# A pairwise attention pooling kernel: Gram rows written 58 wide from a second ScalarE copy, in four DMAs a block in place of eight

## The reference

```
row, col = np.triu_indices(F, k=1)              # 741 pairs of 39 fields
ip = x[:, row, :] * x[:, col, :]                # (B, 741, 64)
hidden = relu(einsum('bpd,da->bpa', ip, W_w) + b_w)
logits = einsum('bpa,a->bp', hidden, W_h) + b_h[0]
a = softmax(logits, axis=1)[:, :, None]
return sum(a * ip, axis=1) @ W_p + b_p          # (2048, 1), float32
```

## Time and profile before

| | |
|---|---|
| median of 3 runs | 1045.51 us (1042.35 to 1046.46) |
| the profiled execution | 1050.66 us, of which the span of the core's instructions is 1048.9 us |
| TensorE busy | 1032.0 us (98%) |
| VectorE busy | 981.7 us (94%) |
| ScalarE busy | 870.6 us (83%) |
| GpSimd busy | 420.5 us (40%) |
| granted TensorE clock | 0.998 of full |
| DMA packets, bytes | 413979, 45.63 MB |

### The profile page before, as it was taken

One profiled execution on the slowest core, in us unless ns is written; L12 is line 12 of the kernel. 1 busy time (PEld: TensorE's weight loads), 2 busy tenths in 40 slices (PEclk: granted clock), 3 DMA queues, 4 the chain that ended last, 5 costly groups with the idle time before them and its releaser, 6 DMA issues.

```text
span 1048.9 us, 59118 instructions
## 1 busy us (share of the span) xinstructions
PE 1032.0 (98%) x24849; PEld 481.6 (46%) x24849; DVE 981.7 (94%) x549; ACT 870.6 (83%) x884; POOL 420.5 (40%) x263
## 2 busy tenths in 40 slices
PE   7999999999999999999999999999999999999997
PEld 3445444444554445544455554544444544444542
DVE  8999999999999999999999999999999989999992
ACT  6888887888888888888888888888888888888885
POOL 6253433452334433535333335333433445342331
PEclk9999999999999999999999999999999999999999
DMA  3242243422434234242342523325253242422422
GB/s 52 40 51 43 36 49 42 47 42 37 49 47 49 36 47 47 39 55 32 48 47 35 61 32 50 42 34 59 35 50 47 31 53 40 50 41 37 47 34 26
DMA packets 413979, 45.63 MB, mean 44 GB/s; under 512 B 413915, under 2 KB 413931, under 8 KB 413931
## 3 DMA queue, kind: packets, MB, share of 16 engines
q1 hardware_dynamic: 413611, 45.12, 33.9%
q10 hardware_dynamic: 320, 0.07, 0.0%
HBM read 26.59 MB, written 18.54 MB: 43 GB/s over the span
## 4 chain that ended last, share of the span: by engine, by line
PE 97%; DVE 1%; issue 1%; ACT 0%; DMA 0%; another core or an unknown queue 0%; ACTq 0%; DVEq 0%
PE z L513 61%; PE logits L563 32%; PE z L502 5%; DVE prod L348 1%; DMA first_x_rows<-in_r_x_dram 0%; ACT hidden L431 0%; ACT exps L454 0%; PE logits L553 0%; DVE neg_max L357 0%; DVE weighted L365 0%; PE z L493 0%; PE z L627 0%; DVE x_wide L330 0%; DVE y_all L371 0%
## 5 line engine op out<-in xcount | busy, mean ns | idle before, releaser
L431 ACT ACTIVATE hidden<-z,b_col 128x988 f32<-128x988 f32 x768 | 803.5, 1085 | 149.2 <-PE z L513 145.6
L348 DVE TENSOR_TENSOR prod<-x_wide 128x2964 f32<-128x2964 f32 (+1 forms) x257 | 822.4, 3246 | 2.1 <-PE z L513 1.2
L513 PE MATMUL z<-prod,w_tiles 64*32 64x494 f32 x12288 | 760.4, 576 | 0.3 <-ACT hidden L431 0.2
L292 POOL COPY head_w<-head_cols 128x64 f32<-128x64 f32 x252 | 408.8, 1624 | 604.2 <-PE logits L563 604.0
L563 PE MATMUL logits<-hidden,head_w 64*32 64x371 f32 (+1 forms) x8192 | 442.3, 472 | 5.5 <-PE logits L563 1.8
L513 PEld LDWEIGHTS z<-prod,w_tiles 64*32 64x32 f32 x12288 | 251.1, 106 | 263.6 <-issue 232.7
L563 PEld LDWEIGHTS logits<-hidden,head_w 64*32 64x32 f32 x8192 | 179.1, 106 | 245.5 <-issue 233.9
L319 DVE STREAM_TRANSPOSE x_wide<-x_rows 128x1024 f32<-128x1024 f32 x63 | 78.5, 1246 | 24.4 <-PE z L502 19.1
L502 PEld LDWEIGHTS z<-x_wide,x_scaled 64*39 64x39 f32 x4096 | 45.0, 113 | 40.1 <-issue 40.1
L439 ACT COPY gram_out<-z 103x624 f32<-103x624 f32 x64 | 43.5, 680 | 16.5 <-PE z L502 14.9
L502 PE MATMUL z<-x_wide,x_scaled 64*39 64x39 f32 x4096 | 52.5, 204 | 1.1 <-DVE prod L348 0.6
(11 more groups left out here) (27 smaller groups left out, 29.0 us busy)
## 6 DMA issues: line engine op xcount, KB each, us to landing
x_rows<-in_r_x_dram SPq DMA_DIRECT2D x252, 64.0 KB
gram<-gram_out SPq DMA_DIRECT2D x256, 47.5 KB
gram<-gram_out SPq DMA_DIRECT2D x256, 23.2 KB
values<-gram SPq DMA_DIRECT2D x128, 46.3 KB, 3.5
x_rows<-in_r_x_dram SPq DMA_DIRECT2D x252, 14.0 KB
first_x_rows<-in_r_x_dram SPq DMA_DIRECT2D x2, 78.0 KB
first_x_rows<-in_r_x_dram SPq DMA_DIRECT2D x1, 156.0 KB
w_tiles<-in_L_rec_W_w_dram ACTq DMA_DIRECT2D x4, 16.0 KB, 2.9
```

The costliest lines, as they stand in the source:

```text
L292: nc.gpsimd.tensor_copy(head_w[:, step % BLOCK_STEPS, :, :], head_cols[:, :, at:at + TILE]).then_inc(head_w_ready, 1)
L348: nc.vector.tensor_tensor(out, one, other, ALU.mult).then_inc(ready, 1)
L431: nc.scalar.activation(hidden[:, i, :, CHUNK * k:CHUNK * (k + 1)], z[:, slot_of(j, v), :, 0:CHUNK], ACT.Relu, bias=b_col[:, 0:1]).then_inc ...
L513: last = nc.tensor.matmul(z[col:col + TILE, slot_of(j, v), b, 0:CHUNK], w_tiles[row:row + D, col:col + TILE], prod[row:row + D, i, first:f ...
```

## The change

`gram_out` gets rows of 58 in place of 39. `copy_gram` writes the 39 columns as before and then takes the first 19 of each matrix out of PSUM once more, in a second ScalarE instruction (103 partitions x 304 elements); `z_read` is raised by the second. `write_gram` issues one DMA of rows of 58 for each quarter, 4 a block, and the counts that wait for them go by 4.

```diff
-        gram_out = sb("gram_out", [P, 2, 2, ROW_DUOS, FIELDS])
+        gram_out = sb("gram_out", [P, 2, 2, ROW_DUOS, WIDE])
...
-        GRAM_DMAS = 8
+        GRAM_DMAS = 4
...
-                        rows = gram_blocks[h, u, :, bass.ds(v, 1), :, :]
-                        sp.dma_start(rows[:, :, :, 0:FIELDS],
+                        sp.dma_start(gram_blocks[h, u, :, bass.ds(v, 1), :, :],
                                      gram_out[at:at + FIELDS, slot, u, :, :]).then_inc(gram_written[slot], 16)
-                        sp.dma_start(rows[:, :, :, FIELDS:WIDE],
-                                     gram_out[at:at + FIELDS, slot, u, :, 0:OFFSETS]).then_inc(gram_written[slot], 16)
...
-                nc.scalar.copy(gram_out[0:ROWS, slot, :, :, :],
-                               z[0:ROWS, GRAM_SLOT, :, 0:XCOLS].rearrange("p u (d f) -> p u d f", f=FIELDS)
-                               ).then_inc(z_read, 1)
+                taken = z[0:ROWS, GRAM_SLOT, :, 0:XCOLS].rearrange("p u (d f) -> p u d f", f=FIELDS)
+                nc.scalar.copy(gram_out[0:ROWS, slot, :, :, 0:FIELDS], taken)
+                nc.scalar.copy(gram_out[0:ROWS, slot, :, :, FIELDS:WIDE], taken[:, :, :, 0:OFFSETS]).then_inc(z_read, 1)
```

## The result

The changed kernel takes 1040.35 us (median of 20 runs, 1038.79 to 1042.09), the kernel before 1042.76 us (median of 20 runs beside them, 1041.08 to 1046.46). The ratio is 0.9974, 95% interval 0.9968 to 0.9980: 2.4 us, a quarter of a percent, faster. Two things add up to the miss of 5.2 us. The level was wrong by 2.7 us, since the median of three runs (1045.51) was high for this kernel; and the effect, forecast as 0, was 2.4 us.

What follows compares the result with a forecast made beforehand. TensorE, busy 98% of the span, was taken to bound the kernel. Every term counted 0 on its path, so the forecast was 1045.5 us, no change, with a range of 1041 to 1050 us.

Steps and rivals of the forecast that it cites:

- The level: Starting time without the profiler, median of three runs: 1045.51 us, to which the change's effect of 0 was added.
- The second ScalarE copy: Added 64 times after the Gram copy: 0.42 us each, fits ScalarE's idle hole before chunk 2's relu, costs 0 on the path.
- the 0.39 us ahead of chunk 5: TensorE's slack at chunk 5, which waits for chunk 3's relu: 530.70 against a start at 531.09 us.
- the 20 us of the sum: ScalarE's added busy time from the second copies, overlap taken off: 64 x (0.42 - 0.11) us.
- The sign of 897 us: What would show the forecast right: ScalarE's busy time up by about 27 us to 897 us.
- The first copy: The 39 columns written into rows of 58 with gaps: 0 extra, at most 0.16 us more, still inside the slack.
- Four DMAs less on SyncE: Four fewer Gram write issues a block, x loads 1.8 us sooner; nobody waits for them, gain 0, loss 0.
- the 333700 of the prediction: Sign of a right forecast: queue 1, the data queue, at about 333700 packets.
- Fewer packets: Gram writes from 159744 to 79872 packets; DMA share 27% to 34%, not on the chain, effect 0.
- two windows: Two neighbouring blocks, 15.83 us each at DMA shares 0.57 and 0.26, taken as showing DMA doesn't press on TensorE.
- Rival 2: Faster: TensorE's stalls were DMA's; half of the 14.2 us gone gives 1038.4 us, all 1031.3 us. Chance 7%.
- 14.2 us: Group openings and stalls between first and last Gram copy, beyond 63 steady blocks: the most a change of waits could give back.

Runs made afterwards that it cites:

- wide_4_no_copy: The changed kernel without the second ScalarE copy, columns 39 to 57 of gram_out zeroed once at the start: 1040.63 us, ratio 0.9873.
- wide_8_halves: The changed kernel with each of the 4 whole-row DMAs cut into two of half as many batches, 8 issues a block: 1040.31 us, ratio 0.9872.
- before_x_sooner: The kernel before with SyncE's order changed, x loads placed between two halves of a block's eight Gram writes: 1041.33 us, ratio 0.9882.
- split_4_apart: The kernel of wide_4_split_rows with its 116 B packets 128 B apart in DRAM in place of end to end: 1040.44 us, ratio 0.9872.
- wide_4_split_rows: The changed kernel, 4 DMAs a block, with every row of 58 sent as two 116 B packets end to end in DRAM: 1132.96 us, ratio 1.0759.
- only_39: The kernel before without the four DMAs of 19 columns, leaving 79872 packets of 156 B at 232 B steps: 1040.04 us, ratio 0.9887.
- narrow_8_pitch_64: The kernel before with DRAM rows 64 floats (256 B) apart in place of 58 (232 B), still 8 DMAs: 1040.30 us, ratio 0.9867.
- copy_kept_8_narrow: The changed kernel, second copy kept, with the writes as before: 8 DMAs a block, runs of 39 and 19: 1052.73 us, ratio 0.9998.
- before_pe_by_4: The kernel before with TensorE's loop over single blocks replaced by one over groups of four blocks: 1192.96 us, ratio 1.1326.

## Why the prediction was wrong, by its steps

**The second ScalarE copy: right.** 0.42 us, in the hole, 0 on the path; wide_4_no_copy has the same time as after. The relu behind it started at its old distance of 1.17 us from chunk 2 in every block, so the 0.39 us ahead of chunk 5 weren't touched. ScalarE's busy time went up by the 20 us of the sum, to 890.3 us. The sign of 897 us at the end of the prediction contradicts that sum, as it counts 64 x 0.42 us without the overlap.

**The first copy: right.** Gaps cost 10 ns (0.69 for 0.68 us).

**Four DMAs less on SyncE: right for whole rows.** Eight or four issues, x loads early or late make no difference there (wide_8_halves, after). With the narrow rows of before the order of the issues is worth 13 us (before_x_sooner). The queue has 330411 packets and not the 333700 of the prediction: each of the 256 issues left out took 13 packets of 4 B with it, 3328 in all, and wide_8_halves, which kept its issues, has 333739.

**Fewer packets: this step failed.** "I take 0 from both ends" rested on two windows with the same 15.83 us at a DMA share of 0.57 and of 0.26. They showed that in these two blocks the loads of `values` didn't disturb TensorE. They did not show that the Gram writes don't, as both blocks contain those, and both happened to be undisturbed. Traffic was weighed by its share of the engines, where kind and place mattered: split_4_apart and wide_4_split_rows have the same packets by number and size, and are 92 us apart. What stood in the place of this 0: with two narrow packets a row at 232 B steps, written by eight DMAs in one go, single x packets take up to 0.8 us and TensorE has late starts; with whole rows there are no such packets, and one late start is left. That is 11 us of late starts in the profiled execution, 2.4 us by the medians of 20 runs, and 10 to 14 us in the later sets.

**Rival 2** was nearest to what happened, with 7%: the late starts were of DMA's making. Its reason (half of the packets) holds only at this step of rows: only_39, with half of the packets, is fast, but so is narrow_8_pitch_64 with all of them. The Trainium skill (DMA: Bandwidth & Descriptors, Rules for kernel authors) says to coalesce small transfers, and the direction came out by it. The runs don't bear it out as the reason here, since narrow_8_pitch_64 coalesces nothing, and wide_8_halves makes DMAs of 35.3 KB in place of 70.7, and both are as fast as after. The same page (Specifications) has DMA do a read-modify-write below 512 B. All Gram packets here are below that, and those at steps of 128, 256 and 512 B cost TensorE nothing; so that rule alone doesn't tell the kernels at 1040 us from those at 1048 us and more.

**The sum and the range.** The other term that was off is the level: 1045.51 us, the median of three runs, where 20 runs gave 1042.76. It makes 2.7 of the 5.2 us of the miss, and no mechanism is in it. The range reached to a third of the stalls' worth below a level that came from three runs with 4.1 us between them. The prediction had noted that the profiled execution lay above all three, and that 14.2 us were not steady pace, and gave the cause of these no chance beyond 7%. Not all of the 14.2 us were stalls either: in after 1001.1 - 63 x 15.83 = 3.8 us of them are left, and each group opening takes some 0.4 us.

**What stays open.** By which path TensorE is held up isn't shown. Its operands don't come from DRAM, its code is resident by the instruction packets, and the profile names only "remote", "issue" or its own logits. That the long x packets and the late starts share a cause rests on their coming and going together from kernel to kernel; within the trace of before they don't coincide. In wide_4_split_rows, the worst of them, 97 of 184 late starts have a long x packet within 1 us, where chance would give 56. Which property of an odd step matters isn't settled either: touching alone doesn't decide, nor does one crossing of 256 B, nor the number of packets at steps of 128, 256 and 512 B. The rate of the writes wasn't varied by itself. In the kernels with other pitches the loads of values read at other steps too; the pair copy_kept_8_narrow and wide_8_halves is free of that. Whether before_x_sooner gains by the pause or by the order of writes and loads wasn't tried apart.

**The best version.** None beat after by more than its scatter. narrow_8_pitch_64 reaches 1040.30 us with ScalarE and SyncE as before; it is the simpler way to the same time. Every version without the disturbance ends at 1040.0 to 1041.3 us, which is TensorE's steady pace but for some 4 us.

## What to carry to other kernels

Time between the first and last of a regular instruction, less the steady pace times the count, is an upper bound of what can be had (here 14.2 us, of which 10.4 came); where the profile names no releaser for it, look at the packets of other transfers in the same stretch before giving it up as scatter. Lay rows that are written to a DRAM scratch tensor in small pieces at a step of 128 or 256 B, even if that leaves gaps: here it cost two constants. Before you test a rate, read from the trace that it changed. To say that DMA doesn't disturb an engine, compare blocks with and without the DMA in question, many of them, and not two windows that both have it.

## What the runs showed of the hardware that was not expected

- The same 159744 packets of 116 B: 1133 us at steps of 116 B, 1040 us at steps of 128 B (wide_4_split_rows, split_4_apart); the mean packet of the queue 23.1 against 13.8 ns.
- One kernel, unchanged, took 1042.8 us in one set of runs and 1050 to 1055 us in the others, with a steady pace that is the same in the traces of both (15.82 us a block); the versions with whole rows took 1040.1 to 1040.6 us in all.
- All packets of before at their old places, with the x loads between the two halves of the Gram writes: 1041.3 in place of 1054.7 us.
- A loop body of one block on TensorE needed 6 instruction packets in all, one of four blocks 229, and the kernel took 140 us more (before_pe_by_4); the granted clock fell from 0.998 to 0.952 with the idle times.
